# Reordering the edges of a fused linear-attention and MLP kernel: way into attention, group edges, last step, final pieces

## The reference

```
xn = layernorm(x)
s  = attention(xn)            # linear attention, 16 query heads, 4 key/value heads of 128
g  = silu(mlp(xn))            # gate/up/down, 512 -> 1536 -> 512, weights rounded to fp8
x  = x + s * g

# attention, per head h with lam = 2**(-8(h+1)/16), over 2 windows of 1024 tokens:
q, k = rope(xn wq), rope(xn wk);  v = xn wv
o[i] = sum over j <= i of exp(-lam (i - j)) (q_i . k_j) v_j      # written in chunks of 64
s = o wo
```

## Time and profile before

| | |
|---|---|
| median of 3 runs | 910.53 us (909.95 to 910.64) |
| profiled execution, its span | 909.1 us, 907.3 us |
| TensorE (PE) busy | 890.6 us, 98% of the span |
| VectorE (DVE), ScalarE (ACT), GpSimd (POOL) busy | 634.6, 421.8, 367.1 us |
| steps of attention, from one key transposition to the next | 35.8 us ordinary, 36.1 to 36.2 us up to that of a group edge |

### The profile page before, as it was taken

One profiled execution on the slowest core, in us unless ns is written; L12 is line 12 of the kernel. 1 busy time (PEld: TensorE's weight loads), 2 busy tenths in 40 slices (PEclk: granted clock), 3 DMA queues, 4 the chain that ended last, 5 costly groups with the idle time before them and its releaser, 6 DMA issues.

```text
span 907.3 us, 12407 instructions
## 1 busy us (share of the span) xinstructions
PE 890.6 (98%) x4104; PEld 738.4 (81%) x4104; DVE 634.6 (70%) x905; ACT 421.8 (46%) x709; POOL 367.1 (40%) x271
## 2 busy tenths in 40 slices
PE   5999999999999999999999999999999999999997
PEld 4888888888888887888888888888888888888886
DVE  7878652676653256766787867678767678788796
ACT  3643443443433446344455444464554545634541
POOL 1011112122122474535456455355454563553544
PEclk9999999999999999999999999999999999999999
DMA  6792304378850524413333413145243043265482
GB/s 212 228 360 108 104 13 161 140 256 311 298 204 10 209 92 143 170 33 154 138 117 140 183 61 140 62 151 204 81 162 129 33 178 142 97 232 163 150 265 71
DMA packets 51115, 138.55 MB, mean 153 GB/s; under 512 B 4224, under 2 KB 25344, under 8 KB 45696
## 3 DMA queue, kind: packets, MB, share of 16 engines
q1 hardware_dynamic: 51072, 138.00, 43.1%
HBM read 96.04 MB, written 41.94 MB: 152 GB/s over the span
## 4 chain that ended last, share of the span: by engine, by line
PE 66%; issue 17%; POOL 13%; DVE 2%; ACT 1%; DMA 0%; POOLq 0%; SPq 0%; DVEq 0%; ACTq 0%
PE bank L1226 65%; POOL d_r L1174 8%; POOL rot L1183 5%; PE bank L1273 1%; DMA stage<-in_x_nat 0%; DVE d_sb L1004 0%; ACT gout L540 0%; PE bank L1382 0%; DVE d_sb L1050 0%; DVE tail_sb L1084 0%; DVE tail_sb L1086 0%; POOL fsplit L1155 0%; DVE acc L1080 0%; DVE rot L990 0%; DVE stats L763 0%
## 5 line engine op out<-in xcount | busy, mean ns | idle before, releaser
L1226 PE MATMUL bank<-xn,aw 128*128 128x512 f32 x960 | 228.6, 389 | 0.0
L1183 POOL TENSOR_TENSOR rot<-rot 128x512 f32<-128x512 f32 x80 | 127.0, 1588 | 237.5 <-DVE rot L991 237.5
L1226 PEld LDWEIGHTS bank<-xn,aw 128*128 128x128 f32 x960 | 179.3, 188 | 36.6
L1226 PE MATMUL bank<-o_r,ow 128*128 128x512 f32 (+1 forms) x792 | 186.1, 385 | 0.0
L1174 POOL TENSOR_TENSOR d_r<-d_sb,d_r 128x512 fp32r<-128x512 f32 x128 | 167.4, 1335 | 38.9 <-ACT d_r L684 38.9
L1226 PE MATMUL bank<-xn,gu_w 128*128 128x512 f32 x768 | 179.9, 389 | 0.0
L1226 PEld LDWEIGHTS bank<-xn,gu_w 128*128 128x128 f32 x768 | 144.2, 188 | 30.1
L1226 PEld LDWEIGHTS bank<-o_r,ow 128*128 128x128 f32 x792 | 144.4, 188 | 28.5
L990 DVE TENSOR_TENSOR rot<-bank,rope 128x512 f32<-128x512 f32 x80 | 55.1, 689 | 94.8 <-ACT rot L664 94.5
L684 ACT CAST d_r<-d_sb 128x512 fp32r<-128x512 f32 x128 | 79.0, 621 | 86.2 <-DVE d_sb L1050 65.3
L663 ACT COPY rot<-bank 64x512 f32<-64x512 f32 x80 | 46.7, 584 | 144.8 <-PE bank L1226 144.3
(11 more groups left out here) (77 smaller groups left out, 942.9 us busy)
## 6 DMA issues: line engine op xcount, KB each, us to landing
xn<-xn_split SPq DMA_DIRECT2D x15, 2048.0 KB, 7.7
v_decayed<-vd_split SPq DMA_DIRECT2D x32, 512.0 KB, 3.6
vd_r<-v_decayed SPq DMA_DIRECT2D x16, 1024.0 KB, 7.1
v_r<-v_split SPq DMA_DIRECT2D x16, 512.0 KB, 5.9
wst<-in_mlp_w SPq DMA_DIRECT2D x10, 768.0 KB, 5.3
xn_split<-xn SPq DMA_DIRECT2D x3, 2048.0 KB, 10.8
stage<-in_attn_w SPq DMA_DIRECT2D x4, 1280.0 KB, 5.7
stage<-in_x_nat SPq DMA_DIRECT2D x16, 256.0 KB, 4.4
```

Of the source, the lines that this page charges most:

```text
L1183: pool.tensor_tensor(rot1[:, r % RRING, :], rot1[:, r % RRING, :], rot2[:, r % RRING, :], ALU.add).then_inc(qk_sum, 1)
L1226: last = pe.matmul(dst, a, b, start=start and x == 0, stop=stop and x == len(pairs) - 1)
```

## The change

It touches four places; the computation stays the same apart from the order of additions in the last three pieces.

Way into attention: the fourth `gates` activation goes behind `st_round`; VectorE does `decay_block(0, 0)` ahead of `st_rest(0)`; GpSimd does `fuse_rest(first + 10)` ahead of the last rotation's addition.

```diff
-            def gates(s):
+            def gates(s, d0=0, d1=KT):
...
-                for d in range(KT):
+                for d in range(d0, d1):
...
                 st_round(n)
+                for other in beside.get("block", ()):
+                    other()
                 decayed_round(n, SC)
...
-                            "state": [lambda: gates(NB - 1)]})
+                            "state": [lambda: gates(NB - 1, 0, KT - 1)],
+                            "block": [lambda: gates(NB - 1, KT - 1, KT)]})
...
             rotate(0, 0)
             projections(0, 0, 0)
+            decay_block(0, 0)
             st_rest(0)
-            for t in range(HEAD):
+            for t in range(1, HEAD):
                 decay_block(0, t)
...
-                            4: [lambda: fuse_rest(first + 8), lambda: fuse_rest(first + 9)],
-                            QK: [lambda: fuse_rest(first + 10), lambda: fuse_rest(first + 11)]})
+                            4: [lambda: fuse_rest(first + 8), lambda: fuse_rest(first + 9), lambda: fuse_rest(first + 10)],
+                            QK: [lambda: fuse_rest(first + 11)]})
```

Group edges, ScalarE and in the same way VectorE (`aw_split_lo`, `rotate`, `o_rest`):

```diff
                 if edge:
                     aw_split_hi(g + 1, 1)
-                elif not last:
+                if not last:
                     turn(n + 1, 0)
                 for i in range(2, NOT):
-                    o_round(n, i)
+                    o_round(n, i, last)
                 if edge:
                     aw_split_hi(g + 1, 2)
-                    turn(n + 1, 0)
```

```diff
+        def o_bank(i, last):
+            return bank[4] if last and i == NOT - 1 else o_ps[i]
-        tail_ps = [bank[5], bank[0], bank[4], bank[1], bank[2], bank[6]]
+        tail_ps = [bank[5], bank[0], bank[3], bank[1], bank[2], bank[6]]
+        SHORT = 3
+        ON_DVE = 3
...
+            def last_rest(n, e):                       # VectorE, behind the decay blocks, ahead of o_rest
+                dve.wait_ge(d_hi, n * NEL + e + 1)
+                dve.tensor_tensor(d_r[:, slot(e), 1, :], d_sb[:, slot(e), :],
+                                  d_r[:, slot(e), 0, :].bitcast(F32), ALU.subtract).then_inc(last_lo, 1)
...
-                if t == NBL - 1:
+                if t == NBL - 1 and last:
+                    pe.wait_ge(acc_d, n * KT + KT)
+                elif t == NBL - 1:
                     pe.wait_ge(o_lo, n * NOT + 1)
-                pe.wait_ge(d_lo, n * NEL + e + 1)
+                if last and t == ON_DVE:
+                    pe.wait_ge(last_lo, 1)
+                elif last and t > ON_DVE:
+                    pe.wait_ge(d_lo, n * NEL + e)
+                else:
+                    pe.wait_ge(d_lo, n * NEL + e + 1)
...
+                if last:
+                    for t in range(HEAD, NBL):
+                        scores(n, t)
+                    for t in range(NBL):
+                        times_v(n, t, last=True)
+                    last_out_projection(n)
+                    return
```

```diff
+            def ahead(k):                              # GpSimd, behind its two finish()
+                u, cols = TAIL[k]
+                x, gate = tail_in(u)[:, 0, cols], tail_in(u)[:, 1, cols]
+                pool.wait_ge(tail_ld[u], 32)
+                pool.tensor_tensor(acc[:, NB - 1, u, cols], acc[:, NB - 1, u, cols], gate, ALU.mult).then_inc(pre_p, 1)
+                pool.wait_ge(pre_p, k - SHORT + 1)
+                pool.tensor_tensor(x, acc[:, NB - 1, u, cols], x, ALU.add).then_inc(pre_d, 1)
...
+            def short_piece(k):                        # VectorE
...
+                dve.wait_ge(tail_out, k + 1)
+                dve.wait_ge(pre_d, k - SHORT + 1)
+                dve.tensor_tensor(gate, tail_ps[k][:, 0:width], gate, ALU.mult).then_inc(tail_p, 1)
+                dve.wait_ge(tail_p, k + 1)
+                dve.tensor_tensor(x, gate, x, ALU.add).then_inc(tail_d, 1)
...
                 if last:
-                    for k in range(len(TAIL)):
+                    for k in range(SHORT):
                         tail_piece(k)
+                    for k in range(SHORT, len(TAIL)):
+                        short_piece(k)
                     return
...
                     for u in (KT - 2, KT - 1):
                         finish(n - 1, b - 1, u)
+                    for k in range(SHORT, len(TAIL)):
+                        ahead(k)
```

More of the change, by code:

```diff
@@ L243, in attention_mlp_kernel @@
         fin_p = sem("fin_p"); fin_d = sem("fin_d")
+        last_lo = sem("last_lo"); pre_p = sem("pre_p"); pre_d = sem("pre_d")
         tail_out = sem("tail_out"); tail_acc = sem("tail_acc"); tail_p = sem("tail_p"); tail_d = sem("tail_d")
@@ L706, in projections, with o_round @@
                 st_round(n)
+                for other in beside.get("block", ()):
+                    other()
                 decayed_round(n, SC)
-            def o_round(n, i):
+            def o_round(n, i, last=False):
                 act.wait_ge(d_used, n * NEL + SC + ODONE[i] + 1)
@@ L713, in o_round @@
                 hs, qs = OTILES[i]
-                act.copy(o_r[:, 0, hs, qs], o_ps[i][:].rearrange("p (h c) -> p h c", h=hs.stop - hs.start)).then_inc(o_hi, 1)
+                act.copy(o_r[:, 0, hs, qs], o_bank(i, last)[:].rearrange("p (h c) -> p h c", h=hs.stop - hs.start)).then_inc(o_hi, 1)
             def step(n, g, b, start=False, edge=False, final=False, last=False):
@@ L1051, in decay_block, with o_rest @@
                                   decay[:, h0:h0 + nh, i0 - j:i0 - j + ni, :], ALU.mult).then_inc(decayed, 1)
-            def o_rest(n, i):
+            def o_rest(n, i, last=False):
                 dve.wait_ge(o_hi, n * NOT + i + 1)
                 hs, qs = OTILES[i]
-                dve.tensor_tensor(o_r[:, 1, hs, qs], o_ps[i][:].rearrange("p (h c) -> p h c", h=hs.stop - hs.start),
+                dve.tensor_tensor(o_r[:, 1, hs, qs], o_bank(i, last)[:].rearrange("p (h c) -> p h c", h=hs.stop - hs.start),
                                   o_r[:, 0, hs, qs].bitcast(F32), ALU.subtract).then_inc(o_lo, 1)
@@ L1072, in finish @@
                 dve.tensor_tensor(fin[:, u, 0, :], fin[:, u, 1, :], fin[:, u, 0, :], ALU.add).then_inc(fin_d, 1)
+            def last_rest(n, e):
[4 more added lines that the diff above has]
+                u, cols = TAIL[k]
+                width = cols.stop - cols.start
+                x, gate = tail_in(u)[:, 0, cols], tail_in(u)[:, 1, cols]
[4 more added lines that the diff above has]
+                dve.tensor_tensor(x, gate, x, ALU.add).then_inc(tail_d, 1)
             def tail_piece(k):
@@ L1097, in step @@
                         aw_split_lo(g + 1, 0)
+                if last:
+                    last_rest(n, SC + ON_DVE)
                 for i in range(2):
@@ L1101, in step @@
                     aw_split_lo(g + 1, 1)
-                elif not last:
+                if not last:
                     rotate(n + 1, 0)
                 for i in range(2, NOT):
-                    o_rest(n, i)
+                    o_rest(n, i, last)
                 if last:
-                    for k in range(len(TAIL)):
+                    for k in range(SHORT):
                         tail_piece(k)
+                    for k in range(SHORT, len(TAIL)):
+                        short_piece(k)
                     return
@@ L1196, in finish @@
                 pool.tensor_tensor(fin[:, u, 0, :], fin[:, u, 1, :], fin[:, u, 0, :], ALU.add).then_inc(fin_d, 1)
+            def ahead(k):
+                u, cols = TAIL[k]
+                x, gate = tail_in(u)[:, 0, cols], tail_in(u)[:, 1, cols]
+                pool.wait_ge(tail_ld[u], 32)
+                pool.tensor_tensor(acc[:, NB - 1, u, cols], acc[:, NB - 1, u, cols], gate, ALU.mult).then_inc(pre_p, 1)
+                pool.wait_ge(pre_p, k - SHORT + 1)
+                pool.tensor_tensor(x, acc[:, NB - 1, u, cols], x, ALU.add).then_inc(pre_d, 1)
             def step(n, g, b, start=False, edge=False, final=False, last=False):
                 for t in range(HEAD, NBL):
-                    decayed_rest(n, SC + t)
+                    if not (last and t == ON_DVE):
+                        decayed_rest(n, SC + t)
                 if last:
@@ L1429, in scores, with times_v @@
                                                for a, c in SPLIT]).then_inc(score_d, 1)
-            def times_v(n, t):
+            def times_v(n, t, last=False):
                 j, h0, nh, i0, ni = BLOCKS[t]
@@ L1442, in times_v @@
                         tile = o_ps[x][:].rearrange("p (h c) -> p h c", h=2)[:, :, P:HALF]
-                        last = products(tile, pairs(slice(x * HALF, (x + 1) * HALF)), start=False, stop=True)
-                    last.then_inc(d_used, 1)
+                        done = products(tile, pairs(slice(x * HALF, (x + 1) * HALF)), start=False, stop=True)
+                    done.then_inc(d_used, 1)
                 else:
                     x = OF_BLOCK[t]
```

(7 more changed lines are left out.)

1 line of the change is left out of this document (removed).

## The result

The changed kernel takes 907.96 us in the median of 9 runs (906.62 to 908.76), the kernel before, in runs beside it, 910.49 us (909.39 to 911.01). The ratio is 0.9973, 95% interval 0.9964 to 0.9981: 2.5 us or 0.27% faster. The profiled execution took 907.59 us, its span 905.8 us.

The account below looks back on a forecast made before the run. TensorE, busy 98% of the span at full clock, was taken as the bound, so only its standstills could be won. Terms 1.4 + 0.9 + 0.35 = 2.65 us off 910.53 gave 907.9 us, range 906.3 to 909.6.

Parts of the forecast that it names:

- (a): Way into attention: reordering on GpSimd, VectorE and ScalarE removes most TensorE waits; gain 1.4 us, bounds 0.9 and 1.7.
- (b): Group edges: the transposition stops waiting for the key's rotation, a smaller wait for weight tile 2 appears; gain 0.9 us.
- the sign to look for: Group edges: 5.6 to 5.75 us between projection pair and output projection, the wait now at the second projection.
- (c): Last step: scores in one run, block 3's low half on VectorE; TensorE's end moves 0.9 us earlier, bounds 0.5 and 1.3.
- (d): Final pieces: GpSimd's added work makes VectorE take turns, giving back what (c) won; (c) and (d) together bring 0.35 us.
- Rival 3: Final pieces: GpSimd starves VectorE by always retaking the port; end 3.3 us later, 911.5 us in all; chance 0.05.
- Rival 1: Final pieces: VectorE keeps up with TensorE, waits for GpSimd falling into gaps; gain 4.25 us, 906.3 us; chance 0.15.
- Rival 2: Waits return one operation later, edges cost 0.2 each, no gain at the end; 909.1 to 909.4 us; 0.30 with Rival 4.
- Rival 4: Way in: TensorE waits for something else there, leaving 1.25 us gain, 909.3 us; chance 0.30 together with Rival 2.

Follow-up runs that it names:

- the repair: Whole change, plus both splits of weight tile 2 moved ahead of the next key's rotation at the group edges: 907.28 us, ratio 0.9972 to the kernel before.
- the way-in kernel: The kernel before with only the way-in part of the change: ratio 0.9990 to the kernel before, stretch 15.67 us.

## Why the prediction was right

The forecast was 907.9 us, 2.65 us off; measured were 907.96 us and 2.5 us off. The four mechanisms came as forecast. That the sum came so close is luck in part: the edges brought 0.28 less than forecast, the last step and the pieces together 0.29 more. By its steps:

- **(a) Way in, 1.4.** Measured 1.42: 0.56 at `down` (forecast 0.5), 0.28 at the state (0.2), 0.58 at the first decayed block (0.7), alone 1.37. The wait forecast at the state, for a low half at 0.4 after it is due, is the one that remained.
- **(b) Edges, 0.9.** Measured 0.62: the mechanism held, the size did not. The new wait was placed rightly: at the second edge the addition ended 2.14 us after the pair's start (forecast 2.13), the low half 0.54 later. Its load was due at 2.50. At the first edge it came at 2.64, late by 0.14, and cost 0.04 (0.04 to 0.08 over five executions). At the other two it came at 2.81, 0.13 behind the low half's end (607.30 at the second) instead of 0.06, late by 0.31, and cost 0.21 and 0.24. I had taken 0.07 for each, out of 0.05 to 0.2 that didn't reach as far, and the sign to look for, 5.6 to 5.75 us, failed at these two edges (5.79 and 5.82). What takes the load 0.13 there is open. That the wait is all there is to it the repair showed: with it gone the three pairs take 5.58.
- **(c) Last step, 0.9.** Measured 0.80: 7.00 us to the output projection, forecast 6.9. The cost of moving the low half to VectorE, GpSimd held for one operation, came as worked out: GpSimd's five take 6.77 us, against 7.55 for six.
- **(d) Pieces.** The step most open to doubt: that GpSimd's extra work would make VectorE take turns and give back most of (c). With turns, VectorE's end was to fall 2.5 us behind TensorE's; it fell 2.20 behind: of the 0.55 that the turns were to give back they took 0.17. (c) and (d) together 0.64, forecast 0.35. The order of the turns was right one by one, their lengths were too long: counted from the start of the output projection, VectorE finished piece 0 earlier than forecast by 0.1 us, piece 2 by 0.25 and the last piece by 0.4. The forecast's turns are in the trace: piece 1's operations 1.00 and 1.40 us, piece 2's 1.25 and 1.11. GpSimd's 256-column addition, taken as 0.72, took 0.74 where nothing held it. By the Trainium skill ("SBUF — State Buffer", section "Who interferes with whom") a VectorE instruction with two SBUF inputs contends with a GpSimd instruction that reads SBUF, and one with at most one SBUF input does not. The traces agree: in these tails VectorE's operations with one input in PSUM kept their 0.41 to 0.43 us (256 columns) and 0.68 to 0.70 us (512) beside GpSimd. Rival 3, one engine winning again and again, didn't appear in any of these tails.
- **The other rivals.** Rival 1 needed the waits hidden; the kernel with PSUM intermediates shows what that would have given: 0.92 instead of 2.20 us behind TensorE. Rival 2's price at the edges was nearly paid, but not its others. Rival 4 is excluded by the way-in kernel.

The scatter of the front part was not in the forecast: it has no step in it, and moves single executions by as much as the parts do.

## What to carry to other kernels

Work moved to an idle engine ahead of time is not free if it shares a port with the engine it relieves: here it cost 0.17 us, and brought 1.15 once VectorE's intermediates stayed in PSUM. When an operation is moved ahead on a hand-ordered engine, work out for the one it passes when it is now ready and when it is wanted; here that was the whole remaining loss at the edges. When a forecast of several terms meets its sum, compare the terms: here two misses of 0.3 us cancelled. With effects of 0.1%, read the stretches, each against the same stretch, and use the total only to see that nothing is given back.

## What the runs showed of the hardware

- VectorE and GpSimd took strict turns, one instruction each, in all the tails where both had two-SBUF-input work queued: no instruction of VectorE took longer than 1.41 us there.
- Writing to PSUM in place costs VectorE hardly anything: 0.70 us for 128x512 and 0.43 for 128x256, against 0.69 and 0.42 to SBUF.
- A weight load that is late costs TensorE less than its lateness at these three places: 0.14 late cost 0.04 to 0.08, 0.31 late cost 0.20 to 0.24 (five profiled executions with this code).
